# Four stages with counters from zero, a fed router stage, spread mixing, and quantising ahead of norms

## The chip, the cores and the metric

The kernel runs on one core of a Trainium2 chip. The metric is the device time of one execution in microseconds; lower is better. TensorE is called PE in the profile, its weight loads PEld, VectorE DVE, ScalarE ACT, GpSimd POOL, SyncE SP.

## The reference

Two transformer layers over a residual of 8 x 256 tokens with 512 features. Cut to what matters:

```python
def reference(x, ctx, ...):
    x = x + attention_over_context_and_cache(layernorm(x), ctx, wq, wk, wv, wo)       # stage a0
    x = x + bitlinear_ffn(layernorm(x), gate, val, out)                                # stage f0
    x = x + grouped_attention(layernorm(x), ctx, Wq, Wk, Wv, Wo, rms norms of q and k) # stage a1
    x = x + moe(layernorm(x), router, 8 experts top 2, shared expert)                  # stage r
    return x

# bitlinear: a token's row is scaled by 127 / its largest element and rounded, the weights are ternary
# moe, on h = layernorm(x):
    probs = softmax(h @ router_w.T); two largest, renormalised
    moe_out = sum over e of combine[:, e] * ((silu(h @ gate_w[e]) * (h @ up_w[e])) @ down_w[e])
    shared  = silu(h @ s_gate_w + s_gate_b) * (h @ s_up_w + s_up_b) @ s_down_w + s_down_b
```

## The kernel before

The residual X stays on chip as 16 tiles of 128 tokens. The work is cut into five stages, each a `Phase` with its own semaphores and instruction block: a0 (first attention), kv (keys and values of the second attention beside the ternary weights), f0 (first feed-forward, `ffn0`), a1 (second attention, `attention1`) and r (`feed_forward1`, router and experts). float32 products are made of three fast products of high and low halves (`matmul3`, lines 70 to 72), so every operand is split: ACT copies the high half, DVE or POOL subtracts it to get the low half. The order of work on each engine is written out by hand; semaphores carry every dependence.

`Phase.start` (lines 44 to 48) raises each semaphore of the stage by one on POOL and then holds all engines at a barrier; every wait is written `at(count)`, which is `count + 1`.

In f0, iteration n of DVE's loop (17 or more iterations, a token tile each) does the four value quarters `val`, the largest elements of the gated row h (`largest_half`), the quantised row `quantised_h(n - 1)` (line 1085, tile f_hq) that PE transposes next, the quantised input `quantised_x`, and, in every fourth iteration, the four layernorms (`norm`, line 1025, tile f_xn) of a later group of tiles; in the iteration after that one `largest` (line 1031) and `scales` of the group.

In a1 there are 64 units (4 head groups x 4 chunks of 512 tokens x 4 heads); after each fourth unit `project` and `add` (line 1474) bring the chunk into X.

Stage r begins with loads on SP (router weights, biases, the first half of the shared expert). DVE takes the statistics of all 16 tiles (lines 116 and 119), ACT the square root, DVE the reciprocal, then `norm` (line 2039, tile r_xn) makes rows that PE transposes (line 2362), ACT and DVE split (lines 1944 and 2045) and SP stores. The first half of the shared expert runs on them: `shared_gate`, `shared_up`, `shared_hidden` (lines 2059, 1965 and 2062: h, its high and low half), `shared_down`, `add` (line 2070). Between them PE makes the router's logits (`logit_rows`, `logit` line 2377). DVE works out which token goes to which expert, 39 tiles of routed tokens follow, and their results go to memory (y_routed). At the end the second half of the shared expert runs over four chunks of four tiles. In a chunk DVE does three `shared_hidden`, then `combine` of its four tiles (line 2112: adds the two routed rows of each token, weighted), then `add` of its four tiles. POOL gathers the routed rows for `combine` (line 1914, tiles e_yg) into two sets of buffers, so the gathers of tile t wait for `combine(t - 2)`. PE's second pair of `shared_down` products waits for the first `add`.

## Time and profile before

| what | value |
|---|---|
| median of 3 runs | 2006.66 us (2004.11 to 2007.76) |
| the profiled execution's own time | 2005.23 us |
| its span | 2003.5 us |
| PE busy, share of the span | 1787.8 us, 89% |
| DVE, ACT, POOL busy | 1239.0, 893.9, 566.6 us |
| mean granted clock of PE | 0.948 of full |

Busy shares are averages over stages with different limits; matmuls are pipelined, so PE's busy time overlaps itself. Windows and timelines of a stretch say more. Stage a0 takes the first 327 us, kv to 476, f0 to 747, a1 to 1429, r to the end, its tail from 1853.

### The profile page before, as it was taken

Reading aid. Unit: us, or ns where it says so; the run is one execution under the profiler, and the core shown is the slowest. Engines: PE = TensorE matmul, PEld = TensorE weight load, DVE = VectorE, ACT = ScalarE, POOL = GpSimd, SP = SyncE. Lnnn points to the kernel's source line nnn. Section 1 sums busy time; section 2 is a strip of 40 time slices with the busy share of each in tenths; the row PEclk is TensorE's granted clock in tenths of the full one; section 3 lists DMA queues with packets and bytes.
Section 4 is the critical chain, followed back from the end, with each engine's and each line's share of the span. In section 5 each row is a group of like instructions: output and inputs, shape, how many; then the busy total and the mean of one; then the engine's idle time right before and its main releaser. Section 6 shows DMA issues by size and latency. Waiting matters only on the chain. (4 is left out here: it accounts for less than half of the span.)

```text
span 2003.5 us, 27862 instructions
## 1 busy us (share of the span) xinstructions
PE 1787.8 (89%) x10226; PEld 1475.0 (74%) x10226; DVE 1239.0 (62%) x2350; ACT 893.9 (45%) x1664; POOL 566.6 (28%) x412
## 2 busy tenths in 40 slices
PE   4999996884899948999999999999499999999876
PEld 4898994772344527888888888888367799999655
DVE  5334333776788736767776777767547577777333
ACT  3233331674566625445554555545231366555110
POOL 1111111221655612122221221211040255554221
PEclk9999998997899978999999999999789999999888
DMA  5000013452011143122221222110161578887432
GB/s 207 25 31 31 22 51 119 156 209 106 1 32 33 43 149 104 54 74 95 85 74 53 75 97 83 53 53 1 49 252 44 168 254 279 287 278 258 137 119 91
DMA packets 127651, 217.02 MB, mean 108 GB/s; under 512 B 8358, under 2 KB 68006, under 8 KB 125350
## 3 DMA queue, kind: packets, MB, share of 16 engines
q1 hardware_dynamic: 117644, 181.11, 26.6%
q0 software_dynamic: 9888, 34.35, 5.6%
q8 instruction: 71, 1.16, 0.2%
q14 instruction: 48, 0.39, 0.1%
HBM read 171.65 MB, written 43.78 MB: 108 GB/s over the span
## 5 line engine op out<-in xcount | busy, mean ns | idle before, releaser
L1312 POOL TENSOR_TENSOR a_rq<-a_ssq,a_mhalf 128x4 f32<-128x4 f32 x64 | 65.1, 1017 | 413.6 <-DVE a_ssq L1434 413.6
L70 PE MATMUL bank<-a_xT_hi,a_wq_lo 128*128 128x512 f32 (+1 forms) x384 | 144.6, 376 | 21.7 <-PEq L48 18.1
L1395 ACT ACTIVATE a_pT_hi<-bank 128x512 fp32r<-128x512 f32 x128 | 69.6, 598 | 192.9 <-PE bank L1549 192.9
L1389 ACT ACTIVATE a_scores<-a_scores,a_nmax 128x256 f32<-128x256 f32 x256 | 127.2, 503 | 27.9 <-DVE a_nmax L1449 27.6
L71 PE MATMUL bank<-a_xT_lo,a_wq_hi 128*128 128x512 f32 (+1 forms) x384 | 139.0, 362 | 0.0
L72 PE MATMUL bank<-a_xT_hi,a_wq_hi 128*128 128x512 f32 (+1 forms) x384 | 139.0, 362 | 0.0
L70 PE MATMUL bank<-a_wo_hi,a_oT_lo 128*128 128x512 f32 x320 | 128.2, 401 | 2.7 <-DVE a_oT_lo L369 1.4
L72 PE MATMUL bank<-a_wo_hi,a_oT_hi 128*128 128x512 f32 x320 | 126.5, 395 | 0.0
L71 PE MATMUL bank<-a_wo_lo,a_oT_hi 128*128 128x512 f32 x320 | 126.4, 395 | 0.0
L1442 DVE SCALAR_TENSOR_TENSOR a_scores<-bank,a_rq,a_mask 128x256 f32<-128x256 f32 x256 | 106.1, 477 | 32.4 <-PE bank L72 24.1
L1861 POOL TENSOR_TENSOR e_wg_lo<-raw_g,e_wg_hi 128x1408 fp32r<-128x1408 f32 x26 | 90.9, 3497 | 123.6 <-ACT e_wg_hi L1928 123.5
L933 POOL TENSOR_TENSOR f_h<-f_vv,f_gs 128x512 f32<-128x512 f32 x64 | 90.7, 1418 | 100.2 <-DVE f_vv L1064 97.0
L70 PE MATMUL bank<-a_pT_hi,a_V_lo 128*128 128x256 f32 x384 | 109.4, 285 | 5.9 <-DVE a_pT_lo L1463 4.3
L1474 DVE TENSOR_TENSOR X<-X,bank 128x512 f32<-128x512 f32 x64 | 44.0, 687 | 106.5 <-PE bank L72 106.1
L72 PE MATMUL bank<-a_pT_hi,a_V_hi 128*128 128x256 f32 x384 | 108.5, 283 | 0.0
L71 PE MATMUL bank<-a_pT_lo,a_V_hi 128*128 128x256 f32 x384 | 108.4, 282 | 0.0
L70 PEld LDWEIGHTS bank<-a_xT_hi,a_wq_lo 128*128 128x128 f32 x384 | 74.4, 194 | 31.5 <-issue 22.5
L1463 DVE TENSOR_TENSOR a_pT_lo<-bank,a_pT_hi 128x512 fp32r<-128x512 f32 x128 | 82.1, 682 | 18.3 <-ACT a_pT_hi L1395 18.3
L1458 DVE TENSOR_SCALAR a_scores<-a_scores,a_rden 128x256 f32<-128x256 f32 x256 | 85.8, 398 | 2.3
L72 PEld LDWEIGHTS bank<-a_xT_hi,a_wq_hi 128*128 128x128 f32 x384 | 73.9, 192 | 11.4
L1449 DVE TENSOR_REDUCE a_nmax<-a_scores 128x2 f32<-128x512 f32 x128 | 81.2, 676 | 0.0
L71 PEld LDWEIGHTS bank<-a_xT_lo,a_wq_hi 128*128 128x128 f32 x384 | 74.3, 194 | 9.0
(402 smaller groups left out, 5457.1 us busy)
## 6 DMA issues: line engine op xcount, KB each, us to landing
raw_g<-in_egw SPq DMA_DIRECT2D x26, 704.0 KB, 4.6
raw_u<-in_euw SPq DMA_DIRECT2D x26, 704.0 KB, 6.2
a_xT_hi<-x1T_hi SPq DMA_DIRECT2D x16, 1024.0 KB, 6.0
a_xT_lo<-x1T_lo SPq DMA_DIRECT2D x16, 1024.0 KB, 8.3
raw_d<-in_edw SPq DMA_DIRECT2D x26, 512.0 KB, 5.7
y_routed<-m_y SPq DMA_DIRECT2D x39, 256.0 KB, 6.1
raw_d<-in_edw SPq DMA_DIRECT2D x26, 192.0 KB, 6.8
a_cTraw<-in_ctxT SPq DMA_DIRECT2D x8, 512.0 KB, 3.5
```

The source lines that it names most:

```text
L70: pe.matmul(out, w[1], x[0], start=first, stop=False)
L71: pe.matmul(out, w[0], x[1], start=False, stop=False)
L72: return pe.matmul(out, w[0], x[0], start=False, stop=last)
L933: pool.tensor_tensor(h[n % 2][:, j * 512:(j + 1) * 512], vv[u % 2][:], gs[u % 2][:], ALU.mult).then_inc(s_h, 1)
L1312: pool.tensor_tensor(rq[:, h % HG, :], ssq[:, h % HG, :], mhalf[:], ALU.pow).then_inc(s_rq, 1)
L1389: act.activation(row, row, ACT.Exp, bias=nmax[:, i % 2, t:t + 1], accum_out=den[:, i % 2, t:t + 1]).then_inc(s_exp, 1)
L1395: act.activation(pT[b].hi[:], ptb[b][:].rearrange("p (k s) -> p k s", k=QT), ACT.Copy).then_inc(ft.hi, 1)
L1442: dve.scalar_tensor_tensor(sc[i % 2][:, r, :], scb[b][:, t * S:(t + 1) * S], rq[:, i % HG, r:r + 1], mask[:, t, :], ALU.mult, ALU.add).the ...
L1449: dve.tensor_reduce(nmax[:, i % 2, b * QT:(b + 1) * QT], sc[i % 2][:, b * QT:(b + 1) * QT, :], AX.X, ALU.max, negate=True).then_inc(s_nmax, 1)
L1458: dve.tensor_scalar(row, row, rden[:, i % 2, t:t + 1], None, ALU.mult).then_inc(s_p, 1)
L1463: dve.tensor_tensor(pT[b].lo[:], ptb[b][:].rearrange("p (k s) -> p k s", k=QT), f32(pT[b].hi[:]), ALU.subtract).then_inc(ft.lo, 1)
L1861: pool.tensor_tensor(pairs[w % 2].g.lo[:], raws[raw_of(w)].g[:], f32(pairs[w % 2].g.hi[:]), ALU.subtract).then_inc(s_glo, 1)
```

## The change

It has five parts.

- **Semaphores.** Only a0 still raises its semaphores, one after the other over all five engines; the other stages count from zero, `at` is gone from their waits, and a wait for zero is not issued (`after`).
- **f0.** `quantised_h(n - 1)` comes right behind `val(n, 1)`, ahead of `norm` and `largest`. The four norms of a group are spread over the iteration.
- **a1.** A region at the top of SBUF (`Last`) holds the first half of the shared expert's gate and up weights, the router weights and the biases. SP loads them at the start of a1 instead of in r. In the last head group DVE takes the layernorm statistics of the 12 tiles of the first three chunks, behind unit 1 of the following chunk, and POOL their inverse deviation by a power.
- **r, head.** DVE starts with the norms of chunk 0. The statistics of the last four tiles come behind the first eight norms, and POOL makes their inverse deviation between `gate_lo(0)` and the low half of the up weights. `logit_rows(0)` runs ahead of the first gate product and each later one right behind its gate product; the last down weights are split later.
- **r, tail.** `combine` of a pair of tiles is put behind single `shared_hidden` of the next chunk. Tiles 0, 1, 2, 3, 7 and 11 get the shared part first and are combined afterwards. A tile's store waits for both.

The core of the diff (of waits that lose `at` none is shown):

```diff
     def start(self):
-        for s in self.semaphores:
-            self.nc.gpsimd.sem_inc(s, 1)
+        engines = (self.nc.gpsimd, self.nc.vector, self.nc.scalar, self.nc.tensor, self.nc.sync)
+        for n, s in enumerate(self.semaphores if self.first else ()):
+            engines[n % len(engines)].sem_inc(s, 1)
         self.nc.all_engine_barrier()
+def after(engine, semaphore, count):
+    if count > 0:
+        engine.wait_ge(semaphore, count)
# f0, DVE, iteration n
-                if ahead_of and i == 0:
-                    norm(GROUPS[g][0])
-                    norm(GROUPS[g][0] + 1)
                 if n < T:
                     val(n, 1)
+                if 1 <= n <= T:
+                    quantised_h(n - 1)
                 if ahead_of and i == 0:
-                    norm(GROUPS[g][0] + 2)
-                    norm(GROUPS[g][0] + 3)
+                    norm(GROUPS[g][0])
                 if ahead_of and i == 1:
                     largest(g)
-                if 1 <= n <= T:
-                    quantised_h(n - 1)
...
                     val(n, 2)
+                if ahead_of and i == 0:
+                    norm(GROUPS[g][0] + 1)
+                if n < T:
                     largest_half(n, 0)
+                if ahead_of and i == 0:
+                    norm(GROUPS[g][0] + 2)
                 if n + 2 < T:
                     quantised_x(n + 2)
                 if n < T:
                     val(n, 3)
+                if ahead_of and i == 0:
+                    norm(GROUPS[g][0] + 3)
# a1, SP, ahead of its loop
+            sp.dma_start(last.rw[:], rw_dram).then_inc(last.small_loaded, 16)
+            sp.dma_start(last.sdb[:], sdb_dram.partition_broadcast(P)).then_inc(last.small_loaded, 16)
...
+            sp.dma_start(last.g[:], gw).then_inc(last.weights_loaded, 16)
+            sp.dma_start(last.u[:], uw).then_inc(last.weights_loaded, 16)
# a1, POOL, behind its loop
+            pool.wait_ge(s_lve, 1)
+            pool.tensor_tensor(last.rstd[:, 0:T - CT], last.ve[:, 0:T - CT], last.mhalf[:, 0:T - CT], ALU.pow)
# a1, DVE
+            def statistics(n, c):
+                dve.wait_ge(s_added, (n + 1) * CT)
+                for t in range(c * CT, (c + 1) * CT):
+                    dve.bn_stats(last.stats[:, t, :], X[:, t, :]).then_inc(s_lstats, 1)
+                for t in range(c * CT, (c + 1) * CT):
+                    dve.wait_ge(s_lstats, t + 1)
+                    dve.bn_aggr(last.mv[:, t, :], last.stats[:, t, :]).then_inc(s_lmv, 1)
...
+                if n > (G - 1) * NC and i % HG == 1:
+                    statistics(n - 1, n % NC - 1)
# r, POOL
             gate_lo(0)
+            pool.wait_ge(s_ve, 1)
+            pool.tensor_tensor(rstd[:, T - CT:T], last.ve[:, T - CT:T], last.mhalf[:, T - CT:T], ALU.pow).then_inc(s_rstd, 1)
             pool.wait_ge(s_uhi, 1)
# r, ACT
             gate_hi(0)
-            act.wait_ge(s_mv, T)
-            act.activation(std[:], mv[:, :, 1], ACT.Sqrt, bias=eps[:]).then_inc(s_std, 1)
-            up_hi(0)
             for t in chunk(0):
                 transposed(t)
-            down_hi(0)
+            up_hi(0)
+            logit_rows(0)
# r, DVE
-            layernorm_stats(dve, (s_stats, s_mv), X, stats, mv, T)
-            dve.wait_ge(s_std, 1)
-            dve.reciprocal(rstd[:], std[:]).then_inc(s_rstd, 1)
-            dve.wait_ge(s_rstd, 1)
             for t in chunk(0):
                 norm(t)
+            dve.wait_ge(s_rw, 1)
+            dve.tensor_tensor(rw2[:, :, E:2 * E], rw[:], f32(rw2[:, :, 0:E]), ALU.subtract).then_inc(s_rw, 1)
...
             norm(CT + 3)
+            for t in chunk(NC - 1):
+                dve.bn_stats(stats[:, t, :], X[:, t, :]).then_inc(s_stats, 1)
...
+            dve.tensor_scalar(last.ve[:, T - CT:T], mv[:, T - CT:T, 1], LN_EPS, None, ALU.add).then_inc(s_ve, 1)
# r, PE
+            logit_rows(0)
             for m in range(M):
                 t = CT * (m + 1)
                 shared_gate(m)
-                if m:
-                    logit(m - 1)
+                if m == 0:
+                    logit(0)
+                else:
+                    logit_rows(m)
                 transpose(t)
                 transpose(t + 1)
                 shared_up(m)
+                if m:
+                    logit(m)
                 transpose(t + 2)
                 transpose(t + 3)
-                logit_rows(m)
# r, tail, DVE
+            added_first = (0, 1, 2, 3, 7, 11)
+            mixed_after = {(0, 3): (0, 1, 2), (1, 0): (3, 4), (1, 1): (5, 6), (2, 0): (7, 8), (2, 1): (9, 10), (2, 3): (11,),
+                           (3, 0): (12, 13), (3, 1): (14, 15)}
             for c in range(NC):
                 for m in range(M):
                     shared_hidden(SV + c * M + m)
...
-                for t in chunk(c):
+                    for t in mixed_after.get((c, m), ()):
                     combine(t)
                 for t in chunk(c):
                     add(t, T + NT + t)
+                for t in mixed_after.get((c, M), ()):
+                    combine(t)
# r, tail, SP, ahead of a tile's store
+                    sp.wait_ge(s_mix, (t + 1) * TOP)
```

## Rows read from the trace of the kernel before

**Rows 1.** The page: busy time (share of the span), and the group of POOL's powers.

```profile
PE 1787.8 (89%) x10226; PEld 1475.0 (74%) x10226; DVE 1239.0 (62%) x2350; ACT 893.9 (45%) x1664; POOL 566.6 (28%) x412
...
L1312 POOL TENSOR_TENSOR a_rq<-a_ssq,a_mhalf 128x4 f32<-128x4 f32 x64 | 65.1, 1017 | 413.6 <-DVE a_ssq L1434 413.6
```

**Rows 2.** Line 47 in five windows: ns min/median/max, first and last start in us.

```profile
L47 POOLq EVENT_SEMAPHORE  x44: 17/17/17, 1.8 to 5.2; - x44
...
L47 POOLq EVENT_SEMAPHORE  x42: 17/17/17, 327.8 to 331.0; - x42
...
L47 POOLq EVENT_SEMAPHORE  x45: 17/17/17, 476.5 to 480.2; - x45
...
L47 POOLq EVENT_SEMAPHORE  x30: 17/17/17, 747.2 to 749.5; - x30
...
L47 POOLq EVENT_SEMAPHORE  x76: 17/17/17, 1429.6 to 1435.8; - x76
```

**Rows 3.** Timeline (start, us, engine, [idle before]) at the head of r.

```profile
1440.59 9.58 DVE L116 BATCH_NORM_STATS2 r_stats<-X 128x6 f32<-128x512 f32 x16
...
1451.90 4.75 DVE L2039 TENSOR_SCALAR r_xn<-X,r_mv,r_rstd 128x512 f32<-128x512 f32 x4
...
1452.93 3.44 POOL L1882 TENSOR_TENSOR e_wu_lo<-raw_u,e_wu_hi 128x1408 fp32r<-128x1408 f32 x1 [3.54 <-ACT e_wu_hi L1931]
...
1444.77 1.38 ACT L1928 ACTIVATE e_wg_hi<-raw_g 128x1408 fp32r<-128x1408 f32 x1 [4.32 <-DMA raw_u<-in_euw]
```

**Rows 4.** Timeline of PE at the head of r.

```profile
1452.50 1.97 PE L2362 MATMUL bank<-ident,r_xn 128*128 128x128 f32 x8 [24.64 <-DVE r_xn L2039]
...
1461.11 0.77 PE L70 MATMUL bank<-r_xT_hi,e_wg_lo 128*128 128x512 f32 x1 [1.76 <-issue]
...
1466.06 1.03 PE L2362 MATMUL bank<-ident,r_xn 128*128 128x128 f32 x8
```

**Rows 5.** Windows: PE, PEld, DVE, ACT, POOL busy (instructions), granted clock, DMA share.

```profile
1461.10:1502.70 41.60, 41.54 (x208) 30.70 (x208) 17.07 (x32) 15.71 (x26) 20.17 (x15) 0.94 0.70 278
1853.00:2000.30 147.30, 111.75 (x444) 86.30 (x441) 52.68 (x75) 16.32 (x25) 34.94 (x32) 0.86 0.35 116
...
1920.00:1925.00 5.00, 4.26 (x10) 3.46 (x11) 1.24 (x3) 0.00 (x0) 1.89 (x2) 0.50 0.83 260
```

**Rows 6.** Timelines of DVE, POOL and PE in one chunk of the tail.

```profile
1909.99 3.11 DVE L2112 SCALAR_TENSOR_TENSOR X<-e_yg,weight,X 128x512 f32<-128x512 f32 x4
...
1911.00 1.41 POOL L1914 DMA_INDIRECT e_yg<-y_routed,slot  x1 [24.57 <-DVE X L2112]
1912.71 1.21 POOL L1914 DMA_INDIRECT e_yg<-y_routed,slot  x1 [0.30 <-issue]
1914.23 0.95 POOL L1914 DMA_INDIRECT e_yg<-y_routed,slot  x1 [0.30 <-issue]
...
1920.74 0.77 PE L70 MATMUL bank<-e_wd_hi,r_h_lo 128*128 128x512 f32 x1 [8.77 <-DVE X L2070]
...
1927.62 0.40 PE L70 MATMUL bank<-r_xT_hi,e_wg_lo 128*128 128x512 f32 x1
...
1933.19 0.39 PE L70 MATMUL bank<-r_xT_hi,e_wg_lo 128*128 128x512 f32 x1
```

**Rows 7.** The chain that ended last: a gather of the same chunk.

```profile
1915.48 3.74 DMA e_yg<-y_routed,slot
```

**Rows 8.** Timeline of DVE: the same step of two successive units of a1.

```profile
1372.99 1.66 DVE L1442 SCALAR_TENSOR_TENSOR a_scores<-bank,a_rq,a_mask 128x256 f32<-128x256 f32 x4 [0.74 <-PE bank L72]
...
1380.36 1.66 DVE L1442 SCALAR_TENSOR_TENSOR a_scores<-bank,a_rq,a_mask 128x256 f32<-128x256 f32 x4 [0.75 <-PE bank L72]
```

**Rows 9.** Timeline of PE in f0: two output projections and a transpose of h.

```profile
585.39 3.62 PE L1209 MATMUL bank<-f_wo,f_hqT 128*128 128x512 bf16 x16
...
598.42 3.62 PE L1209 MATMUL bank<-f_wo,f_hqT 128*128 128x512 bf16 x16
...
611.94 1.05 PE L1201 MATMUL bank<-f_identb,f_hq 128*128 128x128 bf16 x16 [1.21 <-DVE f_x1T_lo L1109]
```

More of the change, by code:

```diff
@@ L83, in __init__, with take, pair @@
         self.hi, self.lo = hi, lo
+class Region:
+    def __init__(self, nc, offset):
+        self.nc, self.offset = nc, offset
+    def take(self, name, shape, dt=F32):
+        size = math.prod(shape[1:]) * (2 if dt == BF16 else 4)
+        t = self.nc.alloc_sbuf_tensor_at(name, shape, dt, offset=self.offset)
+        self.offset += -(-size // 32) * 32
+        return t
+    def pair(self, name, shape):
+        return Placed(self.take(name + "_hi", shape, F32R), self.take(name + "_lo", shape, F32R))
 class Ahead:
@@ L90, in __init__ @@
         self.raw, self.ctx, self.raw_loaded, self.ctx_loaded = raw, ctx, raw_loaded, ctx_loaded
+class Last:
+    def __init__(self, mem, sems, T, E, I):
+        M = -(-I // P)
+        self.limit = mem.offset
+        self.g, self.u = mem.take("raw0_g", [P, KD, I]), mem.take("raw0_u", [P, KD, I])
+        self.rw = mem.take("r_rw", [P, KD, E])
+        self.sdb_at = mem.offset
+        self.sdb = mem.take("r_sdb", [P, D])
+        self.gbias, self.ubias = mem.take("r_gbias", [P, 2, M]), mem.take("r_ubias", [P, 2, M])
+        self.stats, self.mv = mem.take("r_stats", [P, T, 6]), mem.take("r_mv", [P, T, 2])
+        self.ve, self.rstd, self.mhalf = (mem.take("r_" + n, [P, T]) for n in ("ve", "rstd", "mhalf"))
+        self.weights_loaded, self.small_loaded = sems("last_weights_loaded"), sems("last_small_loaded")
 class First:
@@ L127, in attention0 @@
     SCALE = float(D) ** -0.5
-    with Phase(nc) as ctx:
+    with Phase(nc, 1) as ctx:
         def sb(name, shape, dt=F32):
@@ L795, in values @@
             def values(t):
[L796 removed]
+                after(pe, s_vf, max(t - 1, 0))
                 for k in range(KD):
@@ L1227, in _, with attention1 @@
                     xT(n + 2)
-def attention1(nc, banks, X, ident, ones, ahead, first, wq1, x1T_dram, wq_dram, wo_dram, k_dram, v_dram, B, S, G):
+def attention1(nc, banks, X, ident, ones, ahead, first, wq1, x1T_dram, wq_dram, wo_dram, k_dram, v_dram, last, last_drams,
+               B, S, G):
     QT = S // P
@@ L1261, in attention1 @@
         oT = pair("oT", [P, HG, C])
+        assert nc.sbuf_base < last.limit - 1024
         ssq = sb("ssq", [P, HG, CT])
@@ L1670, in feed_forward1 @@
         pair0 = expert_pair(mem, "e0")
-        raw0 = expert_raw(mem, "raw0")
+        raw0 = Expert(last.g, last.u, mem.take("raw0_d", [P, M, D]))
         xn_at = mem.offset
@@ L1698, in feed_forward1 @@
         msg = [tile_mem.take(f"m_sg{j}", [P, I]) for j in range(2)]
-        mhf = [tile_mem.take(f"m_hf{j}", [P, M * P]) for j in range(2)]
+        mhf = [mem_of.take(f"m_hf{j}", [P, M * P]) for j, mem_of in enumerate((tile_mem, Region(nc, last.sdb_at)))]
         sb = lambda name, shape, dt=F32: mem.take("r_" + name, shape, dt)
-        rw = sb("rw", [P, KD, E])
+        rw, sdb, gbias, ubias, stats, mv, rstd = last.rw, last.sdb, last.gbias, last.ubias, last.stats, last.mv, last.rstd
         rw2 = sb("rw2", [P, KD, 2 * E], F32R)
@@ L1734, in feed_forward1 @@
         tsum, rsum = sb("tsum", [P, T]), sb("rsum", [P, T])
-        assert mem.offset <= nc.sbuf_base and tile_mem.offset <= nc.sbuf_base
+        assert mem.offset <= limit and tile_mem.offset <= limit
         expert, tile_ids = row_ids[:, 0:E], row_ids[:, 0:NT]
@@ L2290, in _ @@
                     norm(t + CT + 3)
-            logit(M - 1)
             logit(M)
@@ L2485, in _ @@
                 shared_up(m)
+                if m:
+                    logit(m)
                 transpose(t + 2)
                 transpose(t + 3)
-                logit_rows(m)
-            pe.wait_ge(tr.lo, at(2 * CT))
             shared_gate(M)
-            logit(M - 1)
             logit_rows(M)
```

671 lines of the change are left out of this document (337 added, 334 removed).

## The prediction

> **What bounds the kernel now.** I read the page first: PE is busy for 89% of the span [rows 1], so what can be won lies where PE stands still, and the change must be judged by such places. The 50 us windows show them: the borders between stages, the first 25 us of r, and the tail from 1853 us on. Then came the semaphore line in the windows of the borders [rows 2], the timelines of the head of r for each engine [rows 3, 4], and windows, timelines and the chain of waits of the tail [rows 5 to 7]. The reader is to see three things. At each border POOL raises 30 to 76 semaphores one by one while every other engine is held at the barrier behind it [rows 2]. At the head of r, PE waits 24.6 us for its first transpose and its first real product starts at 1461.1 [rows 4]; from there to 1502.7 it is busy throughout [rows 5]. In the tail PE spends 147.3 us [rows 5] on 441 matmuls that at full pace take 102; once in each of four chunks it stops for some 9 us until the first add, which stands behind four combines that wait for gathers [rows 6, 7].
>
> **Semaphores.** The raising takes 3.2, 3.7, 2.3 and 6.2 us from first to last start in kv, f0, a1 and r, some 0.08 us each, so with the last one 3.3 + 3.8 + 2.4 + 6.3 = 15.8 us [rows 2]. Nothing runs beside it, for POOL arrives at the barrier last. In a0 the 44 raises take 3.5 us [rows 2]; over five engines there are 9 for each, at POOL's pace 0.7 us, so 2.7 us go. Together **18.5 us**. Bounds: 15.8 if a0 gains nothing, 19.3 if its rest vanishes too. What would still hide it is a load in flight across the barrier; the first instructions behind the borders start right at the release, or wait for loads that SP issues behind it.
>
> **f0.** Iterations without norms take 13.03 us on PE with no idle time [rows 9]. Iteration 8 has its four norms ahead of `quantised_h`, and PE then idles 1.21 us for next_lo, which stands behind that [rows 9]; iteration 4 has the same order and idles a little less. With three norms moved behind it, some 2 us are off DVE ahead of the wait, and both idle times go: 2.2 us. Iterations 5 and 9 idle about as long behind `largest`; there h and largest only change places ahead of next_lo, so nothing is won. The norms land later ahead of `quantised_x`, in an iteration in which DVE has over 3 us to wait. Against it: in iteration 1 the rounded row is not ready when DVE would have begun `largest`, so the swap idles it some 0.7 us. I take **1.5 us**, between -1 and 3.
>
> **a1.** The loads (1.4 MB of weights) leave SP's queue ahead of the key loads of the second chunk, which are used some 40 us later. They cost nothing; without that cover it would be the 4 us that raw weights wait for in r [rows 3]. The statistics do cost. A unit takes 7.37 us, and DVE waits only 0.74 us for PE in it [rows 8]. Four statistics are 4 x 0.60 [rows 3] and four aggregations 0.3, so 2.7 us in one go, 2.0 more than the slack. Queued behind them are square_sums, for which POOL's power waits, and the low half of the probabilities, for which PE's `output` waits. That half is ready roughly 1 us ahead of PE. So some 1 us of the 2.0 reaches PE, three times: **-3 us**. Bounds: 0, if PE's queue covers it as it covers `add`, and -6.
>
> **Head of r.** Count from the release of the barrier, 1436.1 before, 0.3 us behind the last raise [rows 2]. Gone: the loads, 16 statistics, square root and reciprocal ahead of the first norm (15.8 us). Now DVE starts norms at 0.1, about 0.5 each (two ended before POOL began [rows 3]). ACT ends the gate weights' high half at 1.7; POOL's low half runs 3.4 us to 5.1. DVE's next subtraction on SBUF tiles, the router's low half, is held until then, as two of the four norms were held in the 4.75 us beside POOL's 3.44 us [rows 3].
>
> The Trainium skill (SBUF — State Buffer, SBUF: two separate sides) says that such a DVE instruction and a GpSimd one exclude each other for a whole instruction. The rows agree; without the lock the sum below would be some 3 us better.
>
> Then, with 0.6 for each low half and 1 for each pair of PE and ACT steps between, chunk 0 is transposed and split at 9.7. `logit_rows(0)`, 8 matmuls at 0.43 us (12 took 4.95 us at 1461.1, at the lower clock [rows 4]), ends at 13.3. The clock rises after about as long as before, so the gate product ends at 16.6. Ready at that time is the up weights' low half? Norms 4 to 7 end at 10.7, four statistics and aggregations at 13.4, the shift at 13.7, POOL's power (1.0 us [rows 1]) at 14.8, the low half (3.4 us) at 18.3; PE asks for it at 18.5, behind logit(0) and two transposes. No stall, but by 0.2 us. The rest is PE's old work: before, the 41.6 us from the first gate product to the last logit [rows 5] contained 4.95 of that product and 1.9 of logit_rows(0), so 34.6 remain, and the head ends at 16.6 + 34.6 = 51.2 instead of 66.6: **15.4 us**. Bounds: 12 (the low half 3.4 us late, or a store of a normed row holding norm 4) and 18. The router behind it is the same work in the same order.
>
> **Tail.** PE's own work: 24 matmuls take 1933.19 - 1927.62 = 5.57 us [rows 6], 0.232 each, so 441 take 102.3. The order now: adds of chunk 0 first, so PE doesn't wait there at all. Combines of a pair of tiles are 3.1 us of DVE [rows 6], beside 2.1 for a hidden product's halves; both fit into 5.57. The gathers are the limit: each pair starts when the buffers come free, four issues with pitches 1.71, 1.52, 1.25 and 1.25 [rows 6], each landing 3.7 us after its issue [rows 7]. I walked through DVE's, POOL's and PE's orders with these durations. Combine 2 stands ahead of hidden (1, 0) and waits for gathers that start with combine 0; that delays 3 and 4, those 5 and 6, and hidden (1, 2) is split 2.9 us later than PE wants it. In chunks 2 and 3, PE waits 0.6 us for the same half, and four times 0.4 for an add. The last add ends 108.7 us after the tail's start; the same walk through the old order gives four waits of 8.9 us and 149.6, against 147.3 in the trace, most of the excess in what it allows for the low clock behind a stop (at 1920 to 1925 it was 0.50 [rows 5]). So 147.3 - 108.7 = **38.6 us**, of which some 8 us are clock: without long stops PE stays at 2.4 GHz. Bounds: the waits all vanish, 43; landings take 6 us because stores and chunk loads run beside them, 30. The added store wait sits on SP, whose next chunk load has 25 us to spare.
>
> The Trainium skill (SBUF — State Buffer, SBUF: two separate sides) also speaks against this: a gather's descriptors are written by GpSimd, which a DVE instruction can lock out. The rows show something of it: 1.41 and 1.21 us for the issues beside combines, 0.95 otherwise [rows 6]. Were all 28 later issues to take 0.46 more, the tail would be some 3 us longer.
>
> **Sum.** 18.5 + 1.5 - 3.0 + 15.4 + 38.6 = 71.0 us. The profiled execution took 2005.2, so 1934.2; it lies 1.4 below the median of the runs shown, so by the median 1935.6. I say **1935 us**.
>
> **Rivals.**
> - *The gathers set the tail.* DVE waits for a gather in program order, with the next hidden product behind it. By the walk, landings of 6 us instead of 3.7 cost 9 us and 8 us cost 24: 1944 to 1959. For it: the landings now meet other transfers; against it: they do so already.
> - *The low half of the up weights holds PE* in r: POOL's order puts the power, and thus all of DVE's work up to it, ahead. 0.2 us is no margin; every us of DVE costs one: 1938 to 1943.
> - *DVE in a1 has no room*, and the statistics cost 2.7 us and a disturbed order of units each, some 10 us in all: 1942.
> - *The semaphores were hidden*, by loads: at most 10 of 18.5: 1945. Against it: all five engines start behind the release.
> - *Slower than before*: gathers and combines serialise. The seven round trips on two buffer sets then set the tail; to lose 71 us they would need some 16 us a landing where the rows have 3.7. Price at that point: 2006 and up. Nothing in the trace is near.
>
> **How the numbers follow.** My forecast has 0.55, within 1926 to 1943; gathers 0.15, low half 0.12, a1 0.07, hidden semaphores 0.04; better than forecast, by waits that PE's queue absorbs, 0.05; slower or unchanged 0.02. The range 1922 to 1949 leaves out most of the gather case's upper half and the last. What a measurement of this kernel can tell from no change is 0.2%, 4 us; every case but the last is faster by far more: faster 0.97, same 0.01, slower 0.02.
>
> **What would show it.** No line-47 events behind a0, and borders shorter by the amounts above. Transposes of r starting some 1 us behind the release instead of 16.4; the first gate product ending near 16.6; POOL's power ending before PE asks for up. In the tail no PE wait over 4 us, the clock at 1.00 in every window, about 109 us in all, DVE's waits for e_yg in chunk 1. In f0 periods of 13.0 in iterations 4 and 8. The prediction is wrong if landings lengthen, if PE idles in the last head group of a1, or if the clock falls again where PE now has short stops.

## The result and the profile after

The changed kernel takes 1946.2 us in the median (first four executions 1945.8 to 1958.2; two more took 1939.9 and 1957.4) beside 2006.2 before: ratio 0.9715 over all six, 95% interval 0.9672 to 0.9759. A second set of five gave 1944.3 beside 2005.4, ratio 0.9687 (0.9674 to 0.9701). The forecast was 1935 with 1949 as its upper end; the first ratio stands for 0.9715 x 2006.2 = 1949.0. So 57 to 61 us went instead of 71. Some executions stand 12 us above the others, and the one profiled first is such a one (1958.2).

The page, its busy line, which answers to [rows 1]:

```profile
PE 1782.2 (91%) x10202; PEld 1470.8 (75%) x10226; DVE 1248.0 (64%) x2351; ACT 890.7 (46%) x1662; POOL 574.9 (29%) x415
```

PE's work is the same but for a few records, its share went from 89% to 91%. The raising of semaphores (count, ns min/median/max, first and last start) is left in a0 alone, over five engines, where [rows 2] had five borders on POOL:

```profile
L55 POOLq EVENT_SEMAPHORE  x9: 17/17/17, 1.8 to 2.5; - x9
...
L55 PEldq EVENT_SEMAPHORE  x9: 51/51/51, 2.0 to 3.2; - x9
```

The head of r, timelines of PE and then of DVE and POOL, answering to [rows 3, 4]; the barrier is released at 1421.2:

```profile
1421.93 1.97 PE L2433 MATMUL bank<-ident,r_xn 128*128 128x128 f32 x8 [2.65 <-DVE r_xn L2096]
...
1430.72 0.58 PE L2440 MATMUL bank<-r_xT_hi,r_rw 128*16 128x512 f32 x1 [1.70 <-DVE r_xT_lo L2102]
...
1437.43 1.05 PE L2448 MATMUL bank<-r_fold,r_lg 16*128 16x8 f32 x8
...
1480.26 0.61 PE L2440 MATMUL bank<-r_xT_hi,r_rw 128*16 128x512 f32 x1 [12.21 <-DVE r_xT_lo L2102]
```

```profile
1458.57 19.79 POOL L1939 TENSOR_TENSOR X<-X,r_sdb 128x512 f32<-128x512 f32 x16 [8.42 <-DVE r_xn L2096]
...
1464.77 14.14 DVE L2119 TENSOR_TENSOR r_h_lo<-r_hf,r_h_hi 96x512 fp32r<-96x512 f32 x1 [0.70 <-ACT r_h_hi L2021]
```

Up to the first logits it runs as forecast: transposes 0.7 us behind the release, first logit row at 9.5 (forecast 9.7), the product behind the first gate product at 16.2 (gate forecast to end at 16.6). Then a subtraction that takes 0.69 us elsewhere takes 14.14, while POOL adds the shared bias (`sdb`) to 16 tiles; it ends 0.55 us behind POOL's last addition. It is called the hold from here on. PE waits 12.21 us, and the head ends 67.6 us behind the release, no sooner than before.

The tail: PE's waits from 1836 to 1956, then windows (PE, PEld, DVE, ACT, POOL busy, granted clock, DMA share, GB/s):

```profile
PE bank L78 <- DVE r_h_lo L2119: 9.1, 3, 8.0
PE bank L78 <- DVE X L2127: 0.5, 3, 0.2
```

```profile
1836.10:1952.30 116.20, 105.74 (x442) 80.91 (x440) 52.57 (x75) 16.10 (x25) 34.79 (x32) 0.96 0.44 147
...
1885.00:1890.00 5.00, 0.00 (x0) 0.00 (x0) 1.87 (x3) 0.08 (x1) 1.45 (x2) 0.56 1.00 408
1890.00:1895.00 5.00, 3.68 (x9) 2.82 (x10) 2.06 (x3) 0.55 (x1) 0.44 (x1) 0.50 0.31 99
```

147.3 us [rows 5] became 116; the four stops of some 9 us became one of 8.0 us, and only there does the granted clock fall to its lower level, 1.2 GHz. The timelines of SP, DVE and PE and the chain of waits say what it waits for:

```profile
1880.30 0.33 SPq L1862 DMA_DIRECT2D r_xT_hi<-xT_hi  x1
1880.67 0.42 SPq L1862 DMA_DIRECT2D r_xT_lo<-xT_lo  x1
...
1888.47 0.75 DVE L2173 SCALAR_TENSOR_TENSOR X<-e_yg,weight,X 128x512 f32<-128x512 f32 x1 [3.01 <-DMA e_yg<-y_routed,slot]
...
1891.32 0.79 PE L78 MATMUL bank<-e_wd_hi,r_h_lo 96*128 96x512 f32 x1 [8.03 <-DVE r_h_lo L2119]
```

```profile
1880.57 7.88 DMA e_yg<-y_routed,slot
```

The gather of tile 6 leaves 0.3 us behind the load of the last chunk (two transfers of 1 MB) and lands 7.88 us later, where [rows 7] had 3.74. `combine(6)` waits for it, and the third hidden product of the chunk stands behind that.

It is not the only one: the four gathers issued from 1.0 us ahead of that load to 3.1 us behind it land after 5.4, 7.9, 7.9 and 7.1 us. In the kernel before, the same load goes out 3.1 us ahead of the first of a row of gathers. That one lands after 5.0 us, the next ones after 4.0, 3.8 and 3.7 us, so the value of [rows 7] is the last of a falling row and was read 7.6 us behind the load. The distance from the load is not all: 3.1 us behind it a gather took 5.0 us before, and 7.1 here, where the three ahead of it were still under way. The load and the first gather of before (ns of the issue, then us to landing), and all five gathers of the changed kernel from 1877.7 on:

```profile
1907.87 0.33 SPq L1811 DMA_DIRECT2D r_xT_hi<-xT_hi  x1
...
L1914 POOL DMA_INDIRECT e_yg<-y_routed,slot x1: 1405/1405/1405, 1911.0 to 1911.0; - x1
DMA to landing us min/median/max: 5.0/5.0/5.0
...
L1964 POOL DMA_INDIRECT e_yg<-y_routed,slot x5: 946/1083/1314, 1877.7 to 1883.4; - x5
DMA to landing us min/median/max: 3.8/7.1/7.9
```

Stage by stage, in us between the releases of the barriers (head: release to the copy of the last logits; tail: last transpose of routed rows to the last add):

| | a0 | kv | f0 | a1 | r | head | middle | tail |
|---|---|---|---|---|---|---|---|---|
| before | 325.8 | 149.2 | 269.2 | 686.4 | 567.4 | 66.6 | 350.1 | 147.6 |
| counters alone (e4) | 324.6 | 145.4 | 266.2 | 679.6 | 566.7 | 66.7 | 349.7 | 147.2 |
| changed, 1958 us | 325.0 | 145.6 | 263.3 | 683.8 | 534.4 | 67.6 | 346.8 | 116.6 |
| changed, 1947 us (e1) | 325.4 | 145.4 | 264.3 | 685.2 | 521.6 | 53.3 | 347.9 | 117.2 |

Each stage's time contains the raises for the next one; a0 counts from its own release, its own border went from 5.5 to 3.5.

### The profile page after: what moved, and what is told of

Read it like the earlier page. It is cut to its first block and busy times, and to the rows that moved or that the text cites. A ratio compares the mean times of both kernels' runs of the same rounds, so it can differ in the third digit from the quotient of the medians.

```text
span 1955.6 us, 27616 instructions
## 1 busy us (share of the span) xinstructions
PE 1782.2 (91%) x10202; PEld 1470.8 (75%) x10226; DVE 1248.0 (64%) x2351; ACT 890.7 (46%) x1662; POOL 574.9 (29%) x415
## 5 line engine op out<-in xcount | busy, mean ns | idle before, releaser
L1447 ACT ACTIVATE a_scores<-a_scores,a_nmax 128x256 f32<-128x256 f32 x256 | 127.2, 503 | 30.4 <-DVE a_nmax L1507 30.2
L973 POOL TENSOR_TENSOR f_h<-f_vv,f_gs 128x512 f32<-128x512 f32 x64 | 95.6, 1495 | 92.9 <-DVE f_vv L1104 91.4
L78 PEld LDWEIGHTS bank<-a_pT_hi,a_V_lo 128*128 128x128 f32 x384 | 74.3, 194 | 11.9 <-issue 9.0
```

The source lines that it names most:

```text
L78: pe.matmul(out, w[1], x[0], start=first, stop=False)
L973: pool.tensor_tensor(h[n % 2][:, j * 512:(j + 1) * 512], vv[u % 2][:], gs[u % 2][:], ALU.mult).then_inc(s_h, 1)
L1447: act.activation(row, row, ACT.Exp, bias=nmax[:, i % 2, t:t + 1], accum_out=den[:, i % 2, t:t + 1]).then_inc(s_exp, 1)
```

## The experiments

Medians are of four to six executions (the three probes ran once), each set beside the kernel before on the same chip (2004.1 to 2007.3). Unless said otherwise an edit is to the changed kernel.

**e1: the changed kernel again.**

> The changed kernel once more, unaltered, for a second trace and a narrower interval. The executions shown so far lie at 1940, at 1946 and at 1957 to 1958 us, and in the one profiled (1958) a DVE low half of h took 14.14 us while POOL ran its 16 additions of the shared bias into X. Theory, a hold that depends on which instruction of DVE meets the additions: the group near 1946 has a shorter hold, so a trace of that group shows the head of r (release to the end of the last logit) some 12 us shorter, about 55 us instead of 67.6, and everything else alike. Rival, the spread comes from elsewhere (loads, the gathers of the tail): the head is 67 us in each trace and another stretch is 12 us shorter.

1944.3 us (1940.9 to 1947.2). The profiled execution lacks the hold, and the head is 14.3 us shorter. POOL's additions (ns min/median/max) and the two instructions, here and in the execution at 1958:

```profile
L1939 POOL TENSOR_TENSOR X<-X,r_sdb x16: 1263/1286/1745, 1461.8 to 1481.0; 128x512 f32<-128x512 f32 x16
...
1461.84 20.47 POOL L1939 TENSOR_TENSOR X<-X,r_sdb 128x512 f32<-128x512 f32 x16 [8.39 <-DVE r_xn L2096]
...
1468.05 1.84 DVE L2119 TENSOR_TENSOR r_h_lo<-r_hf,r_h_hi 96x512 fp32r<-96x512 f32 x1 [0.70 <-ACT r_h_hi L2021]
```

```profile
L1939 POOL TENSOR_TENSOR X<-X,r_sdb x16: 1258/1268/1297, 1458.6 to 1477.1; 128x512 f32<-128x512 f32 x16
```

In both, DVE starts 6.20 us behind the first addition. In the one, an addition of 1.75 us shows that POOL gave way once and DVE was through after 1.84; in the other no addition exceeds 1.30 and DVE gets in when there is none left. The theory holds for where the 12 us are, not yet for what sets it off.

**e2 and e6: the additions elsewhere.**

```diff
# e2
             pool.wait_ge(s_xn, T)
+            pool.wait_ge(s_logc, NC)
             for t in range(T):
# e6
-            pool.wait_ge(s_xn, T)
             for t in range(T):
+                pool.wait_ge(s_xn, t + 1)
```

> POOL starts its 16 additions of the shared bias only once DVE has copied the last logits. Theory, the hold: no low half of h over 2 us in the head of r, the head ends some 52 to 54 us behind the release as forecast (51.2), and the kernel comes to 1938 to 1942 us with no executions at 1958. Rival, the head is short of time for another reason (norms held by stores of normed rows, the first weights): the head still takes some 60 us or more and the time stays at 1946. A third way: the hold moves behind the logits, onto the chain that finds the two best experts, which has many small DVE instructions; then PE waits there and little is won.

> Each addition of the shared bias waits for its own tile's norm instead of for all 16, so POOL begins about 8 us earlier, behind the down weights' low half. Theory, a hold by chance: some 9 additions lie in the gap in which POOL waited, the last ones wait for norms and leave gaps; no hold of 14 us, 1941 to 1945 us. Rival, DVE loses as much in the new place: the norms and low halves of chunk 2 are held, PE waits for r_xT_lo longer than the 4.0 and 1.7 us of the trace without the hold, and the time is 1947 or more.

Both are slower than 1944.3: 1949.9 and 1947.5 us, with no execution far off (spread 1.9 and 1.7 us). In e2 the head ends at 52.6 but the middle takes 354.5 instead of 347.9: the additions now lie beside DVE's search for the experts, and PE waits 2.5 us for the counts and up to 3.4 for a low half. In e6 the low halves of chunk 2 pay: the head takes 57.6, and PE's longest wait for r_xT_lo before a logit row is 3.7 us instead of 1.7. The third way of e2 and the rival of e6 came true: 20 us of additions on SBUF operands cost 3 to 6 us more in these two places than where the change puts them, when the hold stays away. Ten executions without a hold don't tell whether these places are free of it.

**e3: combines one at a time.**

```diff
-            added_first = (0, 1, 2, 3, 7, 11)
+            added_first = (0, 1, 2, 3, 4, 5, 6, 7, 9, 10, 11)
-            mixed_after = {(0, 3): (0, 1, 2), (1, 0): (3, 4), (1, 1): (5, 6), (2, 0): (7, 8), (2, 1): (9, 10), (2, 3): (11,),
+            mixed_after = {(0, 4): (0,), (0, 5): (1,), (1, 0): (2,), (1, 1): (3,), (1, 4): (4,), (1, 5): (5,), (1, 6): (6,),
+                           (2, 0): (7,), (2, 1): (8,), (2, 4): (9,), (2, 5): (10,), (2, 6): (11,),
                            (3, 0): (12, 13), (3, 1): (14, 15)}
...
-                for t in chunk(c):
+                for i, t in enumerate(chunk(c)):
                     add(t, T + NT + t)
-                for t in mixed_after.get((c, M), ()):
-                    combine(t)
+                    for t in mixed_after.get((c, M + i), ()):
+                        combine(t)
```

> Only the tail is altered: one combine at a time, 0 and 1 between the adds of chunk 0, then five a chunk behind single hidden products and single adds, so that a gather has at least two such places of time. In the trace of the changed kernel the tail takes 116.4 us with one PE wait of 8.0 us for a low half of h, behind combines that waited for gathers. Theory, gathers in program order with combines in pairs cost that wait and the low clock behind it: PE waits under 1 us in all, the tail 108 to 110 us, the kernel 6 to 8 us faster (1938 to 1940). Rival, the transfers of the tail as a whole are the limit (the chunk load at full DMA share): the gathers still land 8 us late there, and a wait of 3 us or more stays.

1932.5 us: five executions from 1929.4 to 1933.1, and one at 1944.2, the profiled one, with a hold of 14.13 us. The tail takes 105.5 us, and PE's waits in it are

```profile
PE bank L78 <- DVE X L2127: 0.7, 4, 0.2
PE bank L78 <- DVE r_h_lo L2119: 0.5, 1, 0.5
```

The gain is 11.8 us, more than the 6 to 8 expected: the 8.0 us, the low clock behind it and the small waits of the other chunks all go. The load stays where it was, and one gather issued 0.7 us ahead of it still lands after 6.3 us, but PE's waits in the tail stay at 0.5 us or less.

**e7: the load behind the gathers.**

```diff
                 if c + 2 < NC:
                     sp.wait_ge(s_u, product_of(SV + c * M + M - 1) + 1)
+                    if c == 1:
+                        sp.wait_ge(s_mix, 7 * TOP)
                     chunk_load(c + 2)
```

> Only the load of the last chunk's input (two transfers of 1 MB) is moved: it waits until tile 6 is combined. In the changed kernel it is issued at 1880.30, beside four gathers, of which the slowest lands 7.88 us after its issue; the DMA share is 1.00 at 1885 to 1890 and PE waits 8.0 us for the low half of h behind it. Theory, the load slows the gathers: none of the gathers ahead of tile 6 lands later than 5 us, PE's wait shrinks from 8.0 to about 3 (2.9 in my walk), and 5 to 7 us go, part of them clock. Rival, the order of the combines alone sets it: the wait stays at 6 to 8 us.

1938.6 us, 5.6 less, with combines and gathers in the changed kernel's order. PE's waits in the tail, and the load:

```profile
PE bank L78 <- DVE r_h_lo L2121: 4.9, 3, 3.0
PE bank L78 <- DVE X L2129: 0.5, 3, 0.2
```

```profile
1869.90 0.33 SPq L1862 DMA_DIRECT2D r_xT_hi<-xT_hi  x1
```

The wait is 3.0 us where the walk through the orders had 2.9. So the order of the walk was right and the constant 3.7 us a landing was wrong beside the load: the theory stands, the rival falls. The tail takes 112.1 us, still 3.4 more than the walk's 108.7. Some 1.7 of them are clock, for even behind this short stop PE takes 0.42 us instead of 0.23 for each of nine products, which the walk left out. The window (PE, PEld, DVE, ACT, POOL busy, granted clock, DMA share, GB/s):

```profile
1871.10:1876.10 5.00, 4.18 (x11) 3.22 (x12) 2.07 (x3) 0.04 (x1) 0.80 (x1) 0.66 1.00 395
```

**e4: the counters alone.** The kernel before, each `wait_ge(s, at(count))` behind a0 made `after(engine, s, count)`, and `start` as in the change.

> The kernel before with the counters from zero alone: only the first attention raises its semaphores, over five engines. My forecast for this part: 18.5 us (15.8 at four borders, 2.7 in the first), so a ratio to before of 0.9908, 1988 us. Rival, part of it was hidden or is given back inside the first attention, which took 2.5 us longer in the changed kernel's trace: 1990.5 to 1991. Rival, half of it hidden by loads: 1996.

1987.1 us, ratio 0.9906 (0.9891 to 0.9921): 18.3 us, with an interval of 3 us to either side. The term was 18.5.

**e10: f0's old order.** The order of the kernel before put back in f0 alone.

> The changed kernel with the old order in the first feed-forward: all four norms and the largest elements ahead of the quantised row. My forecast for this part was 1.5 us between -1 and 3; the stage took 266.2 us with the counters alone and 263.3 to 264.3 in seven traces with the new order, so 2.4 us: I expect the stage at 266 and the kernel 1.5 to 3 us slower than 1944. Rival, the difference belongs to the loads of the next stage and not to the order: the stage stays at 264.

1946.0 us, f0 at 266.7 us. PE's idle time ahead of the transposes of h in iteration 8 is 1.22 us here and 0.19 with the new order; that of iteration 4, 0.97 in the trace of before, is gone. So 2.0 us of the gain are at the two places forecast. The order is worth 2.5 us by the stages (266.2 and 266.7 against 263.2 to 264.7); the totals, 1946.0 and 1944.3, agree within their spread but alone would not show it.

**e8, e9: the statistics in a1.**

```diff
# e8
-                if n > (G - 1) * NC and i % HG == 1:
-                    statistics(n - 1, n % NC - 1)
+                if n > (G - 1) * NC and i % HG < HG - 1:
+                    t = (n % NC - 1) * CT
+                    statistics(n - 1, ((t,), (t + 1,), (t + 2, t + 3))[i % HG])
# e9, in add(n, c), and the power of tiles 8 to 11 made in r with that of 12 to 15
                 for t in range(CT):
+                    if n == G * NC - 1:
+                        tile_statistics((c - 1) * CT + t)
                     dve.wait_ge(s_out, n * CT + t + 1)
```

> The statistics of a chunk in the second attention are spread: one tile behind each of the first two units, two behind the third, instead of four behind the second. The second attention took 679.6 us with the counters alone and 683.8 to 685.2 in four traces with the statistics, 4.2 us more where I forecast 3.0. Theory, DVE has 0.74 us to spare in a unit and loses only what is above it: the cost falls to about half, 681.5 to 682.5, and the kernel gains 2 us. Rival, what DVE does is paid in full wherever it lies: 683.8 as now.

> Spreading the statistics took the cost out of the first two chunks (with the counters alone the last adds of chunks 13 and 14 come 41.2 and 41.1 us behind those before; in the changed kernel 41.8 and 41.7, spread 41.1 and 41.2), but the last chunk stayed at 38.1 to 39.3 us against 34.8. Here the statistics of tiles 8 to 11 stand between the last four adds, where DVE waits for PE, and their power moves into the next stage beside that of tiles 12 to 15. Theory, the cost arises where PE has no other unit to go on with: the last chunk falls back to about 35 us, the stage to about 680.5, and the kernel gains 3 us (1941 on a median of 1944). Rival, the work comes back at the end of the stage or in r, since the wait of DVE for the power is now ahead of the norms of chunk 2: the time stays at 1944.

Neither gains clearly, and both theories missed the stage: 1945.4 and 1942.5 us, the stage at 685.2 and 684.1 (681.5 to 682.5 and 680.5 expected, 679.6 without statistics). The first adds of the last chunks, counted from the stage's release, show more: from the 13th to the 16th the distances are 41.2, 41.1 and 34.8 us in e4, 41.7, 41.7 and 38.3 in e1, 41.2, 41.1 and 39.3 in e8, 41.7, 41.8 and 37.3 in e9, where moreover the last four adds take 8.0 us instead of 7.3 from the first start to the last end (the 7.4 and 5.9 of a later expectation end at different adds). Nearly all arises in the last chunk. The place also differs from execution to execution: e12 has the second attention of e9 unaltered, and its last distance is 34.7 us instead of 37.3. Windows of the last units of the stage in e4 and in e1, placed alike against the stage's end:

```profile
1389.30:1394.30 5.00, 4.61 (x40) 4.44 (x39) 4.96 (x12) 3.65 (x11) 1.01 (x1) 1.00 0.01 3
1394.30:1399.30 5.00, 1.94 (x17) 1.70 (x16) 5.00 (x13) 3.28 (x10) 0.00 (x0) 1.00 0.00 0
1399.30:1404.30 5.00, 4.16 (x21) 3.81 (x22) 3.42 (x10) 2.16 (x5) 0.00 (x0) 0.66 0.00 0
```

```profile
1393.80:1398.80 5.00, 2.98 (x24) 2.56 (x22) 4.96 (x15) 2.78 (x8) 1.01 (x1) 1.00 0.00 0
1398.80:1403.80 5.00, 0.51 (x2) 0.54 (x3) 4.96 (x14) 1.80 (x8) 1.17 (x1) 0.79 0.00 0
1403.80:1408.80 5.00, 4.35 (x22) 3.98 (x21) 2.78 (x8) 1.79 (x3) 1.24 (x1) 0.53 0.00 0
```

There DVE is busy for 4.96 of 5 us and PE is not: no further unit is left for it. Four statistics more make PE's longest wait 6.1 us instead of 3.3, and its clock falls sooner.

**e14: the old tail.** All four combines of a chunk behind its third hidden product, `added_first` empty.

> The changed kernel with the old tail: all four combines of a chunk behind its third hidden product, ahead of its adds. In the traces the tail took 147.3 us before and 116.4 changed, so 31 us where I forecast 38.6. Theory, the parts add up: 1944 + 31 = 1975 us. Rival, a part of the 31 belongs to other edits (the state of the queues at the start of the tail): under 25 us, 1968.

1974.2 us: 1970.3 to 1974.8 in four executions, and two at 1988.1 and 1989.1 that have the size of the hold on top (no trace of them). By the medians the mixing is worth 29.9 us, or 28.9 without these two; the tail takes 146.9 us instead of 117.2 (e1). So the parts add up to within 2 us.

**e5, e11, e13, e15, e16: what holds DVE.**

```diff
# e5
                 pool.tensor_tensor(X[:, t, :], X[:, t, :], sdb[:], ALU.add).then_inc(s_bias, 1)
+                pool.wait_ge(s_bias, t + 1)
# e15
             pool.wait_ge(s_xn, T)
+            pool.memset(last.mhalf[:], -0.5)
# e13, a stage behind the kernel; e11 and e16 are of the same kind
+    for j in range(10):                                                             # POOL, trial k
+        pool.tensor_tensor(X[:, j, :], X[:, j, :], X[:, 15, :], ALU.add).then_inc(s_p, 1)
+        if k % 2 or j == 9:
+            pool.wait_ge(s_p, k * 10 + j + 1)
+    dve.tensor_tensor(row, row, X[0:m, 11, :], ALU.subtract).then_inc(s_r, 1)       # DVE, m 128 or 96
```

> POOL waits for the end of each addition of the shared bias before the next, where they are issued now. The hold of DVE came in two of three traces of this order: 14.14 and 14.13 us for a low half of h until POOL had no addition left, no addition over 1.30 us; in the third the low half took 1.84 us and one addition 1.75 us, though the low half started 6.20 us behind the first addition in all three. Theory, POOL's additions follow each other without a gap and DVE gets in only by chance: with a gap behind each, no low half of h over 2.5 us, no execution near 1957, times as those without the hold, 1941 to 1945. Rival, the length of an instruction decides, not the gap: the hold comes back in some executions (12 us longer) and the median may be 1957.

> One POOL instruction more (writing again a tile of 128x16 constants) between POOL's wait for the norms and its first addition of the shared bias, so that the additions lie some 0.1 to 0.3 us later against DVE. Theory of a narrow window of starts: the low half of h now starts at another place of an addition; it takes the same short time in each execution (0.9 to 1.8 us), no execution near 1957, or the hold comes in all. Theory of chance: it comes as often as before, in 3 of 27 executions so far, so in this number it may well be missing: only a hold in some of the executions would tell. The time without hold is 1944.

> The changed kernel with a stage behind it that measures the hold alone; its time as a whole means nothing. In each of 40 trials POOL does 10 additions of 128x512 (two SBUF operands), and DVE starts one subtraction of the same kind behind the fourth; ACT sets its start 50 elements later in each pair of trials. In the even trials the additions are issued without a wait between, in the odd ones POOL waits for each to end. Theory of chance: in the even trials DVE's subtraction mostly takes 1 to 2 us but in some it takes until POOL has no addition left (5 to 7 us); in the odd ones never over 2.5. Rival, the length of the additions alone decides: both kinds look alike. Second rival, the hold needs other traffic as well: no trial of either kind is over 2.5 us.

> In the first probe DVE's subtraction started 0.1 us or more ahead of the end of the addition beside it and never took over 1.59 us. In the kernel the held low half starts 6.20 us behind POOL's first addition, which is just ahead of the end of the fifth (5 x 1.27 = 6.3). Here 160 trials of 10 additions in four kinds (additions without and with a wait behind each; subtraction on 128 partitions, or on 96 with the half's output type), with DVE's start moved in steps of 12 elements of ACT from 0.15 us ahead of an addition's end to some 0.25 us behind it. Theory, a narrow window of starts near the end of an addition leaves DVE out until POOL has no addition left: some trials without waits take 5 to 7 us, and none of those with a wait behind each. Rival, one more addition at most: no trial over 2.1 us of any kind, and the hold in the kernel needs something that the probe does not have (a third engine on the tiles, the stores).

> A third probe, nearer to the kernel: 160 trials of 16 additions on POOL (in half of them with a wait behind each), beside 48 transposes on PE; DVE makes a row of 96 partitions from a PSUM bank, ACT copies it as high half and then a PSUM bank, and DVE subtracts as in the held instruction; in half of the trials SP stores four tiles meanwhile. DVE's start moves by 32 elements of ACT in each group of four trials. Theory, the hold needs company on the tiles and comes in about one of ten meetings: some of the 80 trials without waits show a subtraction of 4 us or more, none of the 80 with waits. Rival, as in the first two probes: one addition is waited for at most, no subtraction over 2.1 us; then what sets off the hold stays open.

e5: 1942.7 us (1939.8 to 1946.1), the low half 1.11 us. e15: 1945.3 us, the low half 0.69 us, five executions between 1940.2 and 1949.4. The first probe ran otherwise than its expectation says: 48 trials of 16 additions over four tiles, with a wait behind every fourth in the even ones. DVE's subtractions in the three probes (count, ns min/median/max):

```profile
L2708 DVE TENSOR_TENSOR X<-X x48: 834/1214/1594, 1951.7 to 2943.7; 128x512 f32<-128x512 f32 x48
```

```profile
L2712 DVE TENSOR_TENSOR X<-X x160: 686/744/1833, 1948.4 to 4059.8; 128x512 f32<-128x512 f32 x80, 96x512 fp32r<-96x512 f32 x80
```

```profile
L2729 DVE TENSOR_TENSOR Z<-Z x160: 686/1116/1868, 1954.3 to 5293.8; 96x512 fp32r<-96x512 f32 x160
```

In 368 trials DVE waits for one addition at most (1.87 us less its own 0.69), with or without waits on POOL: both rivals "one addition" came true, and a start near an addition's end does not by itself set off the hold. Only 160 of the trials (half of e13 and of e16) have a row of ten or more additions without a wait, so only these could show a hold like that of the kernel; at the kernel's rate some 17 would have, so the probes lack something that the kernel has. In the kernel the hold came in 5 of 48 executions with the additions at the change's place and without waits (two seen in traces, at 1958.2 and in e3; one by its time, 1957.4; two by theirs in e14), and in none of the 15 with a wait behind each (e5, e12, e17). At that rate 15 without one are no rarity (about 0.2), so that the wait cures it is not shown. What sets it off stays open.

**e12 and e17: the best.** e12 joins e3, e5 and e9. e17 spreads the statistics of the first two chunks as e8 does and puts those of tiles 8 to 11 in pairs (the edit against e9's lines):

```diff
                 for t in range(CT):
-                    if n == G * NC - 1:
-                        tile_statistics((c - 1) * CT + t)
+                    if n == G * NC - 1 and t % 2 == 0:
+                        tile_statistics((c - 1) * CT + t)
+                        tile_statistics((c - 1) * CT + t + 1)
                     dve.wait_ge(s_out, n * CT + t + 1)
```

> The changed kernel with three edits: combines one by one, a wait behind each addition of the shared bias, and the last statistics between the last adds of the second attention. From 1932.5 (the first alone) less 3: 1929.5 us, and no execution 12 us above the others. If the edits do not add up, 1932; if the wait of DVE for the power holds the norms of chunk 2, 1932 to 1934.

> The best kernel so far (1931.8 us) with the statistics of the second attention laid anew: those of the first two chunks spread over three units, as where chunks 13 and 14 fell back from 41.7 to 41.2 us, and those of tiles 8 to 11 two ahead of the first and two ahead of the third of the last adds, so that none stands between two adds that PE has ready together (there they made the last four adds take 7.4 us instead of 5.9). Theory, each keeps its gain: 1.0 + 1.4 = 2.4 us less, 1929.4, the stage at 680. Rival, the clock in the last units decides and not DVE's few instructions: the stage stays between 682 and 684 and the time at 1931 to 1932.

e12: 1931.8 us (1931.7 to 1932.1), a1 at 682.5; that is 0.7 us less than e3 alone where 3 were expected, so the gains don't add up. e17: 1925.8 us (1925.4 to 1929.6), ratio 0.9605 (0.9591 to 0.9620), a1 at 679.4, which is the stage without any statistics. That is 6.0 us less than e12 by the medians where 2.4 were expected; the two traces differ by 2.5 (3.1 in a1), and the rest of the 6.0 is not explained. Its windows of the last units are those of e4 again:

```profile
1388.10:1393.10 5.00, 4.62 (x40) 4.44 (x39) 4.96 (x12) 3.65 (x11) 1.29 (x2) 1.00 0.01 3
1393.10:1398.10 5.00, 1.92 (x17) 1.69 (x15) 5.00 (x13) 3.29 (x10) 1.32 (x1) 1.00 0.00 0
1398.10:1403.10 5.00, 4.17 (x21) 3.83 (x22) 3.41 (x10) 2.15 (x5) 0.00 (x0) 0.66 0.00 0
```

So the statistics, placed like this, cost a1 nothing in this trace, the clock included; with e9 and e12 apart by 2.6 us at the same code, one trace doesn't fix the size. The kernel is 18 us faster than the change.

## Why the prediction was right and wrong

**Semaphores**, 18.5 forecast, 18.3 measured (e4). Right: nothing ran beside them, and a row of raises from first to last start was the price.

**f0**, 1.5 forecast, 2.5 measured by the stages (e10), inside its bounds, 2.0 of it in iterations 4 and 8 as said.

**a1**, -3 forecast, -4.2 to -5.6 measured (bounds 0 to -6). The mechanism, queued work behind four statistics, was right, but it was costed as three equal chunks of 1 us. The first two cost 0.5 to 0.6 each and the last 3.5, for there PE has no next unit (e1, e8, e17); the other 1.0 us of e1's 5.6 lies ahead of the first statistics. [Rows 8] are of two units some 60 us ahead of the stage's end, which have successors, and say nothing of its last units.

**Head of r**, 15.4 forecast. Without the hold it is 52.5 to 53.4 us long (forecast 51.2), so 13 to 14 are won: the term was right within its bounds, and the up weights' low half held nothing, as said. Of the 2 us missing, 1.3 are a wait for a low half ahead of a later logit row (e1). With the hold it wins nothing (67.6). The step that failed is "The rest is PE's old work": it took 34.6 us of the stretch of before as a constant (41.6 - 4.95 - 1.9 is 34.75), and in that stretch the third low half meets POOL's additions. It took 1.14 us in the trace of before, where it started 5.7 us behind the first addition; now, 6.2 us behind it, it can take 14; none of the executions of the kernel before shown beside the runs stands apart (2002.0 to 2010.3). The lock was weighed for two instructions at the start and not for 16 in a row. By the Trainium skill (SBUF — State Buffer, SBUF: two separate sides) whoever starts first holds the port for a whole instruction; that is what the 368 trials show (one addition at most). The 14.14 us over some eleven additions go beyond it, and their cause stays open.

**Tail**, 38.6 forecast, 30 to 31 measured, at the lower bound of 30. (The 38.6 set the trace of before against the walk; the walk through both orders gives 149.6 - 108.7 = 40.9.) The step that failed: four gathers of a pair "each landing 3.7 us after its issue", a constant from [rows 7]. The median landing stayed at 3.8, but the four gathers issued around the chunk load took 5.4 to 7.9, and one of 7.88 carried the critical combine: 8.0 us of wait instead of 2.9 (3.0 with the load moved, e7, which gives back 5.6 us). This is the rival "the gathers set the tail", by the few gathers beside a load and not by a mean landing of 6 us; the time it named, from 1944 on, is the time measured. The 0.15 it was given was too little, since the load's place (behind the chunk's last up product) stood in the code, and the first gather behind a load took 5.0 us in the trace of before. A second step failed by less: "without long stops PE stays at 2.4 GHz" does not hold behind a stop of 3.0 us (e7). One by one the tail takes 105.5 us (e3), 2.5 to 4.5 less than expected. The longer issues of the gathers, which the prediction weighed against the tail, did not grow: some 0.95 us in the median and 1.41 at most, before and after. The Trainium skill (SBUF — State Buffer, SBUF: two separate sides) says of DVE's 2-port modes that they keep GpSimd from writing descriptors; whether a combine does so is shown by no run.

**The middle of r**, left at zero, gained 2 us; no run was made on it.

**Sum** by the medians of e4 and the stages of e1, whose trace has no hold: 18.3 + 1.9 - 5.6 + 13.3 + 2.2 + 30.4 = 60.5; measured 61.1 (e1). Of the ten us missing from 71, eight are the tail's. The hold adds 12 to 15 in one of ten executions; two of the first six had it, and that is what took the first ratio from 1944 to the edge of the range. The rivals of hidden semaphores, of the up weights' low half and of a slower kernel fell; the one of a1 had some 10 us where 4.2 to 5.6 were measured.

## What to carry to other kernels

When work is moved to where an engine has slack, read the slack at the very place: the last unit of a pipeline and the moment of a big load have none, though the rows of the middle do. A DMA latency belongs to what else is under way: look up what the queues issue at the same moment, before and after the change, and leave a slot between a gather and its user. If single executions stand apart by a fixed amount, take a second trace before explaining the first.

## What the runs showed of the hardware

- A DVE subtraction with two SBUF operands beside a row of POOL additions without gaps took 14.14 and 14.13 us in two traces, until POOL's last addition, and 0.69 to 1.88 in the others with the same order; 368 trials in three probes never passed 1.87 us.
- Beside a load of 2 MB at a DMA share of 1.00, gathers issued from 1.0 us ahead of it to 3.1 us behind it landed 5.4, 7.9, 7.9 and 7.1 us after their issue. In the kernel before, gathers issued 3.1 to 7.6 us behind the load took 5.0, 4.0, 3.8 and 3.7 us; the median of all 32 is 3.8 in both.
- In the last units of a1 PE's granted clock was 0.53 behind 5 us with 0.51 us of work (e1), and 0.66 behind 5 us with 1.94 (e4): there 3 us of DVE's work cost 3.5. In the tail it was 0.55 over the 3.6 us behind a stop of 3.0 us (e7).
